# Two graph layers with experts on one core: opening, both mixings and the last experts in new orders, some passes moved to GpSimd

## The reference, cut to what matters

```python
x = x + _L0_gnn_ref(_layernorm(x), edge_index, ...)          # 8 heads of 32: h = x @ W.T, softmax over a node's edges, sum of messages, + bias
x = x + _L0_ffn_ref(_layernorm(x)[None], ...)                # 8 experts, one routing for all nodes
x = x + _L1_gnn_ref(_layernorm(x), edge_index, types, ...)   # 4 heads of 64, relations by type:
    msgs = jnp.where(deg[:, None, None] > 0, agg, V)         #   a node without edges takes its own value
    out = msgs.reshape(N, H * D) @ Wo + bo + node_features
    return (out - mean(out)) / jnp.sqrt(var(out) + 1e-05) * gamma + beta
x = x + _L1_ffn_ref(_layernorm(x)[None], ...)                # 32 experts, argmax of logits, relu(relu(x W1 + b1) W2 + b2)
```

## Time and profile before

| | us |
|---|---|
| median of 3 runs | 1889.08 |
| profiled execution | 1889.01 |
| its span | 1887.3 |
| what lies around the span | 1.7 |
| opening, to the first gather of edges | 69.3 |
| first edge stage | 574.4 |
| first mixing | 50.0 |
| routing and first experts | 200.9 |
| projection and second edge stage | 723.6 |
| second mixing | 112.4 |
| placing | 61.3 |
| second experts | 95.3 |

### The profile page before, as it was taken

The page is one execution under the profiler, slowest core; times in us unless marked ns, Lnnn a source line. Parts: engine busy times, 40 slices in busy tenths (PEclk is TensorE's granted clock), DMA queues, the critical chain, the costliest instruction groups (busy, mean ns, idle before and its releaser), DMA issues. The chain is left out here.

```text
span 1887.3 us, 29227 instructions
## 1 busy us (share of the span) xinstructions
PE 1322.0 (70%) x7062; PEld 931.0 (49%) x7062; DVE 1424.9 (76%) x3656; ACT 925.3 (49%) x3196; POOL 1024.1 (54%) x1096
## 2 busy tenths in 40 slices
PE   6436656665675569998866887787877877665087
PEld 5324434443443457776544555555555554454076
DVE  5558888888898953446867999999999997676234
ACT  2445555556455343322440777777777775132043
POOL 2477777777777100000517777777777776100556
PEclk9767877787787759999986899999999998766599
DMA  4456676677676119000458888888888884425392
GB/s 144 145 179 206 208 217 204 204 209 218 199 216 189 57 33 358 3 1 4 141 172 273 268 263 261 267 263 272 263 263 267 268 267 130 141 70 126 141 313 75
DMA packets 168821, 353.59 MB, mean 187 GB/s; under 512 B 27799, under 2 KB 64744, under 8 KB 168532
## 3 DMA queue, kind: packets, MB, share of 16 engines
q0 software_dynamic: 58192, 175.85, 30.9%
q1 hardware_dynamic: 110469, 175.88, 28.6%
HBM read 268.43 MB, written 87.33 MB: 189 GB/s over the span
## 5 line engine op out<-in xcount | busy, mean ns | idle before, releaser
L784 POOL DMA_INDIRECT e_rows<-h_rows,src_col x416 | 413.7, 994 | 163.5 <-issue 121.9
L1302 POOL DMA_INDIRECT e_rows<-kv_rows,src_col x320 | 306.4, 958 | 100.8 <-issue 68.7
L1061 PE MATMUL e_sum<-e_rows,e_of_dst 128*128 128x264 f32 x832 | 294.1, 496 | 88.8 <-DVE e_rows L883 80.1
L1521 ACT ACTIVATE e_rows<-e_rows 128x64 f32<-128x64 f32 x1152 | 281.4, 336 | 0.3
L1584 PE MATMUL e_query<-q,e_to_dst 128*128 x1248 | 203.7, 294 | 75.7 <-DVE e_rows L1355 56.2
L1061 PEld LDWEIGHTS e_sum<-e_rows,e_of_dst 128*128 128x128 f32 x832 | 176.5, 239 | 129.9 <-DVE e_rows L883 83.8
L1624 PE MATMUL e_sum<-e_rows,e_of_dst 128*128 128x260 f32 x640 | 187.4, 416 | 1.9 <-POOL e_rows L1231 1.0
L1584 PEld LDWEIGHTS e_query<-q,e_to_dst 128*128 128x128 bf16 x1248 | 120.8, 100 | 132.0 <-issue 92.5
L986 ACT ACTIVATE e_rows<-e_rows 128x32 f32<-128x32 f32 x832 | 181.0, 305 | 0.1
L1443 DVE TENSOR_TENSOR acc<-acc,e_sum 128x260 f32 x346 | 145.6, 421 | 43.2 <-DVE acc L1443 20.3
L1302 POOL DMA_INDIRECT x<-kv_rows,src_col x96 | 91.6, 954 | 71.5 <-POOLq L2107 39.8
(11 more groups left out here) (423 smaller groups left out, 2697.5 us busy)
## 6 DMA issues: line engine op xcount, KB each, us to landing
step_of<-e_of_dst SPq DMA_DIRECT2D x104, 256.0 KB, 2.2
e_of_dst<-step_of SPq DMA_DIRECT2D x104, 256.0 KB, 3.5
sorted_rows<-zeros SPq DMA_DIRECT2D x1, 14560.0 KB
comb<-sorted_rows SPq DMA_DIRECT2D x56, 260.0 KB, 4.3
e_rel<-step_rel SPq DMA_DIRECT2D x26, 512.0 KB, 4.3
step_to<-e_to_dst SPq DMA_DIRECT2D x26, 512.0 KB, 5.8
e_to_dst<-step_to SPq DMA_DIRECT2D x52, 256.0 KB, 4.4
e_rows<-h_rows,src_col POOLq DMA_INDIRECT x416, 3.3
```

The costliest lines, as they stand in the source:

```text
L784: pool.indirect_dma_start(out=g[t // BATCH % R][:, t % BATCH, :], out_offset=None, in_=k.h_rows[:, :], in_offset=bass.IndirectOffsetOnAxis ...
L1061: pe.matmul(psm[t % NB], of_dst[q][:, s % GROUP, :], g[m % R][:, s, :], start=True, stop=True).then_inc(summed, 1)
L1302: pool.indirect_dma_start(out=rows_at(t, 1)[:, 0, :], out_offset=None, in_=k.kv_rows[:, :], in_offset=bass.IndirectOffsetOnAxis(ap=k.src_c ...
L1521: ins = act.activation(x, x, ACT.Copy, scale=row[:, plo + h:plo + h + 1])
```

## The change

In the opening the loads of `x`, `W` and the attention vectors go from SP's queue to the start of ACT's, which also takes the table of its root early (`warm`). Destinations get a semaphore of their own. DVE's list is reordered, `Norm` is split into statistics and inverse with two buffers, and the `xn` passes of windows 15 to 24 go to GpSimd. `hit` and `tile_g` become bf16 (the latter as two parts), so that L537 is 16 matmuls of one pass, and these go behind window 4 on PE, `columns` to window 20, `rows_over_steps` to window 21.

```diff
+        POOLED = (3, 4)
...
             ends_of_tiles()
-            tiles_of_steps()
+            statistics(0)
             attention_columns()
             normalise(0)
+            tiles_of_steps()
+            statistics(1)
+            normalise(1)
+            statistics(2)
             windows_of_steps()
-            normalise(1)
+            normalise(2)
+            statistics(3)
+            normalise(3)
             rows_of_steps()
-            normalise(2)
+            statistics(4)
+            normalise(4)
             columns_of_steps()
-            normalise(3)
-            normalise(4)
...
+            for r in POOLED:
+                pool.wait_ge(k.dve_steps, marks["inverted", r])
+                pool.wait_ge(x_in[r], 16 if r + 1 < WROUNDS else 32)
+                for j in range(UNR):
+                    w = r * UNR + j
+                    wait(pool, k.tile_turned, before + w + 1 - XN)
+                    norm.apply(pool, xn[:, w % XN, :], k.x[:, w, :], r, j).then_inc(normed, 1)
...
+            ROOTS = {UNR - 1: 1, UNR + 1: 2, 2 * UNR + 1: 3, 3 * UNR + 2: 4}
```

```diff
+        @block.gpsimd
+        def _(pool):
+            for r in range(1, WROUNDS):
+                vals = k.acc0[:, r * UNR:(r + 1) * UNR, 0:D]
+                pool.tensor_tensor(vals, vals, k.acc0_odd[:, r * UNR:(r + 1) * UNR, 0:D], ALU.add).then_inc(joined, 1)
```

```diff
-GROUPS_OF = [(0, 4), (4, 8), (8, 12), (12, 16), (16, 20), (20, WIN)]
+GROUPS_OF = [(0, 2), (2, 6), (6, 10), (10, 14), (14, 18), (18, 22), (22, WIN)]
...
             for r in range(NG):
-                if r + 2 < NG:
-                    message(r + 2)
-                inverse(0, r)
-                apply_first(r)
-                statistics(1, r, lambda w: k.comb[:, w, 0:D])
+                if r:
+                    scale_and_shift(1, r - 1)
+                if r + AHEAD < NG:
+                    scale(r + AHEAD)
                 if r + 1 < NG:
                     add_residual(r + 1)
-                    statistics(0, r + 1, lambda w: z[(r + 1) % 2][:, w - GROUPS_OF[r + 1][0], :])
-                inverse(1, r)
-                second_shift(r)
+                add_features(r)
+                if r + 1 < NG:
+                    scale_and_shift(0, r + 1)
+                v.wait_ge(mixed, r + 1)
+                statistics(1, r, lambda w: k.comb[:, w, 0:D])
```

In the second experts the buffers of results are seven:

```diff
-        IN, HR, OUT, LOAD = WIN, 4, 4, 8
+        IN, HR, OUT, LOAD = WIN, 4, 7, 8
```

## The result

The changed kernel takes 1860.51 us (median of four, 1858.75 to 1861.72), the kernel before 1890.12 over its runs on the same chips; the ratio is 0.9842, 95% interval 0.983 to 0.9854. The forecast was 1858, faster.

A forecast was written before the change was run, and what follows sets the result against it. The mixings were taken as bound by chains through several engines, the second experts by GpSimd's scatters. The terms -10 + 8 - 24.6 - 4.5 = -31.1 against 1889.0 gave 1858 us, range 1836 to 1880.

The forecast's parts named there:

- Opening: Stage before the first edges: PE begins some 14 us earlier, most of it lost; last copy at 55.5, -10 us.
- First mixing: GpSimd's four sums delay DVE's round 0 by 9.8 us, 1.8 comes back; sum +8 us.
- Exclusion: Both mixings: GpSimd passes and DVE passes with two SBUF inputs wait for each other; 4 x 2.45 us in round 0.
- The repayment of 1.8: First mixing: shorter ACT waits and a gain in the last round, less the wider inverse, give -1.8 us.
- Second mixing: Work moved from DVE to ACT and GpSimd shortens the stage from 112.4 to 87.8 us, -24.6.
- The period of 10.0: Second mixing: 10.0 us per group of four instead of 16.8, from GpSimd's 6.4, DVE's excluded 2.46 and 1.1 added.
- the last rival: GpSimd becomes the bound in the mixings: whole -80.9 + 49.8p for price factor p, 1898 at p = 1.8; chance 0.09.
- Second experts: Three more result buffers let scatters come each 1.29 us throughout, limited by busy transfers; -4.5 us.
- No exclusion: Mixings: GpSimd and DVE passes do not hold each other up; sum -48.4, 1841 us; chance 0.15.
- Every DVE pass excluded: Second mixing: statistics too wait for GpSimd, 14.1 us per group, stage +1; 1884 us; chance 0.08.
- TensorE at its low clock: Second mixing: PE still needs 12.3 us a group, so the stage gains only 4.1; 1878 us; chance 0.13.
- GpSimd as the bound: Mixings: slower GpSimd passes set the pace; total even at price factor 1.62, 1898 us at 1.8; chance 0.09.

The follow-up runs named there:

- statistics_ahead: Changed kernel with round 4's statistics moved ahead of the work on the gathered rows in DVE's opening list; 1855.74 us, ratio 0.983.
- no_gpsimd_in_opening: Changed kernel with all normalised windows of the opening on DVE, GpSimd only gathering there; 1859.08 us, ratio 0.984.
- no_gpsimd_in_second: Changed kernel with the second mixing's masking, adding and weighing on DVE, messages two groups ahead instead of three; 1877.97 us, ratio 0.9925.
- four_buffers: Changed kernel with four result buffers instead of seven in the second experts; 1868.12 us, ratio 0.9869.

## Why the prediction was right, point by point

*Opening, -10 forecast, -6.6 measured.* The mechanism held: window 0 began 12.3 us earlier and most of that was lost at round 4's statistics behind `rows_of_steps`; `statistics_ahead` shows it. The size was off ahead of window 20, which was turned at 48.41 and not at 44.5; from there to the last copy it took 10.9 us, as forecast (11.0). "The gathered rows land at about the same 34": DVE had them at 36.96 and was done with them at 42.15, 2.95 later than the 39.2 of the sum. PE had the tile numbers at 21.5, but DVE took them at 26.88, behind round 1's windows and round 2's statistics; the first gather started at 28.41 instead of 27.15 and the rows took 8.6 instead of 7.7 us from there. The rest, some 1.0, is PE's work ahead of window 20 at the granted clock of 0.50. No row showed the 1.5 us for PE's start after a pause; behind the pause PE lost about 2.7 us against the full clock of `no_gpsimd_in_opening` (45.05 to 50.79 against 44.54 to 47.62). And the GpSimd pass was set at 0.6; it took 1.39 beside DVE and 1.21 alone, but no window of the changed kernel waited for it there, and the ten passes cost 0.5 us by what they held up on DVE.

*First mixing, +8 forecast, +8.1 measured.* Exclusion was priced with four times 2.45; the passes took 3.2 each, and round 0 grew by 9.1 over the one without GpSimd (17.9 against 8.8). The repayment of 1.8 came to 1.0. So the mechanism held, and that the sum came out to 0.1 us is luck, as the two errors cancelled.

*Second mixing, -24.6 forecast, -23.1 measured.* The period of 10.0 came out at 10.4 to 10.6, but not from the two engines in turn, so that the near hit is luck in part. GpSimd's passes cost 1.26 times the price taken (47.8 us in all, 13.5 + 10.3 + 19.9 and 2.3 + 1.8 for the group of three, against 37.9 from the rows, 10 passes of 1.96, 2 of 1.47 and 25 of 0.616), and DVE's passes grew by some 9 us in sum over the stage (L2492, L2447 and L2474 in all their shapes, against their lengths in `no_gpsimd_in_second`). Yet GpSimd stood 23.1 us waiting for ACT, and without the weighing on it the stage keeps its length (90.8). What ends the wait of DVE is ACT's root; on ACT's list that stands behind the copies of messages, and these wait for PE, the busiest engine of the period. Whether PE or ACT bounds this chain was not tried. The step that the forecast lacked is the lead: it counted what GpSimd takes off DVE (4.9 us by experiment for the messages) and not how many groups ahead the messages are made (12.8 for one group, with the messages on DVE). By the formula of the last rival a factor of 1.26 gives -18 us in total; -29.6 was measured, as GpSimd was not the bound.

*Second experts, -4.5 forecast, -6.5 measured,* of which 5.1 are the buffers by `four_buffers` and the rest an earlier first scatter (10.2 instead of 11.3 us into the stage). The busy transfers of the earlier trace rows were no limit: at the same share of 0.90 the scatters kept 1.29.

*The sum.* The four terms gave -31.1 and their stages -28.1; opening and second mixing missed one way by 3.4 and 1.5, the second experts the other way by 2.0. The total of 1860.5 lies 2.5 us from the forecast, which is less than two unedited stages vary by, so its closeness proves less than the stages do.

*The rivals.* No exclusion falls with the first mixing. Every DVE pass excluded falls too: statistics kept 0.41 beside GpSimd, and the inverse its 1.40. The Trainium skill, SBUF — State Buffer, Who interferes with whom, has it so for passes with one SBUF input outside certain fast modes; the trace agrees for these two. But scalar passes with one SBUF input were excluded (L1755, 2.82 instead of 0.27), and the trace before the change had a row of that kind, beside the GpSimd pass that starts at 905.68 and takes 3.08; the same pass takes 0.40 elsewhere:

```profile
905.94 2.98 DVE L2252 TENSOR_SCALAR xn<-x,ln_mv,ln_rstd 128x256 f32<-128x256 f32 x1
```

TensorE at its low clock did not happen: the granted clock was 0.83 and 0.82 in the two periods, 0.73 over the stage. GpSimd as the bound did not happen. The Trainium skill, GPSIMD Engine Reference, section 4.1, has GpSimd about twice as slow for two inputs. The runs show 2.45 to 3.2 against 1.49 for the long sum, so 1.6 times alone and 2.1 beside DVE.

## What to carry to other kernels

Price a pass that is moved to GpSimd twice: its own length, and the length of every DVE pass with two SBUF inputs, and of every scalar pass, that it can stand in front of. Put it where DVE waits for something else, not where both engines have work from the same moment, as in the first mixing. Before a pass is moved to another engine, try how far ahead its own engine can make it: one more group of lead was worth 12.8 us here, the other engine 4.9. Look also whether a wait of the first engine has room for it, as one moved line had for 5.2 us. And before a loss is put down to the engine that was given work, look at TensorE's granted clock behind the pause: 2.8 of 3.3 us lay there.

## What the runs showed of the hardware

A scalar pass on GpSimd (subtract and multiply by two values per partition, 128 x 256) took 1.21 us with DVE mostly idle, longer than GpSimd's product of two tensors of that size (0.71 to 0.72 in the later groups) and three and a half times DVE's 0.34 per pass. The Trainium skill, GPSIMD Engine Reference, section 4.1, has passes with one input nearly at line rate; this row differs, and the measurement decides.

A DVE pass of 0.16 us on 128 x 4 elements took 2.10 when it met a GpSimd pass; from the timeline after the change:

```profile
1647.04 3.20 POOL L2533 TENSOR_TENSOR acc<-val,acc 128x1024 f32<-128x1024 f32 x1
1648.16 2.10 DVE L2474 SCALAR_TENSOR_TENSOR shift<-mv,rstd 128x4 f32<-128x4 f32 x1
```

It ends when the GpSimd pass does. So the price of exclusion is up to what is left of the other pass, whatever one's own length. A scalar pass of DVE with one SBUF input is also held up (L1755, 2.82 instead of 0.27), an inverse is not (1.40 in both).
